# The last graph layer's adjacency product in whole fp32 instead of split fp32r

## The chip, the cores and the metric

The kernel runs on one core of a Trainium2 chip. The metric is the device time of one execution in microseconds. The core has TensorE (matrix products), VectorE (DVE), ScalarE (ACT), GpSimd (POOL), SyncE (SP, which here issues most transfers) and 16 DMA engines.

## What is computed

Four graph layers over 4096 nodes with 128 features each, and one dense 4096 x 4096 adjacency matrix `adj`. Each layer is a residual step on `h = relu(layernorm(x))`. The fourth, whose last part this case is about, is:

```
d = 1 / sqrt(sum(A, axis=-1))
z = leaky_relu(d[:, None] * (A @ (d[:, None] * x)) @ W1 + b1, 0.1)
S = exp(-sqrt(max(|z_i - z_j|^2, 0) + 1e-10) / 2), kept for the 4 nearest of each row, else 0
A2 = S + A
out = d2[:, None] * (A2 @ (d2[:, None] * x)) @ W2 + b2, with d2 = 1 / sqrt(sum(A2, axis=-1))
x = x + out
```

So each layer multiplies by `adj` once, and the fourth twice: once for `z`, and once more ("the last layer" below) for `out`, where four gathered neighbour rows are added to each row.

## The kernel before

**Visits.** The adjacency matrix is streamed from HBM in units of 512 KB: 256 rows of the contraction (two k-tiles of 128) by 512 output columns. TensorE's work on one unit is a *visit* (`Visit`, `visit(v)`). The ring in SBUF has `SLOTS` = 10 units; SP loads a unit as soon as TensorE has used the one ten visits before (`load_unit`, semaphore `used`). A block is 512 nodes (`NB` = 8 blocks), and a block of a layer takes `UNITS` = 16 visits, accumulated in one PSUM bank out of four.

**Split and whole.** A *whole* visit multiplies the ring's fp32 data by an fp32 operand (`G_first` or `G_last`) in one matmul per k-tile (line 429; the trace shows two records for one such matmul). A *split* visit has ScalarE round the unit to fp32r (`upper`, A_hi, tile staged in six buffers), VectorE subtract it from the data (`lower`, line 1066, A_lo, written over the ring's slot), and TensorE do three fp32r matmuls per k-tile (lines 424 to 426: hi x hi, hi x lo, lo x hi). The operand is split as well: `G_hi` by ScalarE and `G_lo` by VectorE.

**The search.** Between the product for `z` and the last layer, TensorE computes the 4096 distances of each of 32 row tiles (lines 599 to 603), ScalarE moves them out as `scores` (two halves of 2048, two buffers), and VectorE scans each tile twice (MAX8, line 1142, and FIND_INDEX8, line 1144). Once in four tiles VectorE also does `clamp`, `new_degrees`, `new_inverse` and `last_rest`, and ScalarE `similarity`, `new_roots` and `scale_last`. `scale_last` multiplies the rows `G_last` by the new inverse roots, which is the operand of the last layer; in the kernel before it also makes G_odd_hi, and `last_rest` (line 1169) makes G_odd_lo.

**The last layer.** Its 128 visits start when the last scores are out of PSUM. Block 0 is multiplied whole, since VectorE is still scanning; in blocks 1 to 7 the visits 7 and 15 are whole and the other 14 split, so 98 split visits and 30 whole. `G_last` is stored to HBM (`scaled_rows`), and when the eight stores have landed and the scans are done, GpSimd issues 128 indirect transfers (line 1246), four for each of 32 row tiles, into `landing`, which has slots for eight tiles. ScalarE scales the four rows (`scale_neighbours`, 16 instructions for a block's four tiles), VectorE adds them (`weigh`, lines 1177 and 1179), and this frees the slot. When a block's visits are done, ScalarE moves the bank out (`move_out`, at the fourth visit of the next block in its own order), TensorE transposes it (`natural`, line 462), and VectorE finishes the block's rows (`last_rows`, lines 1185 to 1193). SP stores them.

**Order.** Every engine works in the order in which its instructions are written. `near_due` says behind which visit a tile's `scale_neighbours` and `weigh` stand; it comes from three constants, of which `LAST_US` stands for a visit's time and `NEAR_US` for a tile's gathers. In the kernel before the tiles 27 to 31 fall due behind the last visit.

Of the kernel before, what the change touches and what calls it, by code (L numbers as in the profile page):

```python
# [58 lines left out]

WHOLE_BESIDE_SCANS = tuple(range(UNITS))  # L60
WHOLE_LAST = (7, 15)

LAST_US, NEAR_US, NEAR_FIRST = 1.5, 6.1, 9.0


class Plan:


    def __init__(self):
# [24 lines left out]
        for n in range(UNITS * NB):  # L96
            b, j = n // UNITS, n % UNITS
            u = j if b else (NB - 1 - j // HALVES) * HALVES + j % HALVES
            self.visits.append(Visit(len(self.visits), b, u, (4,), j not in (WHOLE_BESIDE_SCANS, WHOLE_LAST)[b > 0]))
            self.spans.setdefault((4, b, 4), [len(self.visits) - 1, 0])[1] = len(self.visits) - 1  # L100
# [4 lines left out]
        for t in range(NT):  # L105
            at = min(UNITS + int((NEAR_FIRST + NEAR_US * t) / LAST_US), UNITS * NB)
            self.near_due.setdefault(self.rows_end + at, []).append(t)
# [81 lines left out]
def gnn_stack(nc, x_in, at_in, pack_in, scaled_rows, out):  # L189
# [4 lines left out]
    with ctx:  # L194
# [11 lines left out]
        def take(name, kib):  # L206
# [97 lines left out]
            sem("clamp_ready"), sem("dist_ready"), sem("simil_ready"), sem("deg2_ready"), sem("root2_ready"))  # L304
        last_ready, lasthi_ready, lastlo_ready = sem("last_ready"), sem("lasthi_ready"), sem("lastlo_ready")
        zss_ready, negsq_ready = sem("zss_ready"), sem("negsq_ready")
# [65 lines left out]
        def _(pe):  # L372
# [17 lines left out]
            def operand_of(v, q, p):  # L390

                kb = v.u // HALVES
                if q == 0 and v.split:
                    pe.wait_ge(firstlo_ready, NB - 1)
                elif q == 0:
                    pe.wait_ge(first_ready, kb + 1)
                elif q < 4:
                    pe.wait_ge(g_ready, nth_h(q - 1, kb) - NB)
                elif v.b == 0:
                    pe.wait_ge(lastlo_ready if v.split else last_ready, NB - kb)  # L400
                else:
                    pe.wait_ge(lastlo_ready, NB)

            def visit(v):
# [11 lines left out]
                for q in v.feeds:  # L416
                    acc, odd = ps[:, PLAN.bank[q, v.b, p], :], 1 if q == 4 else q % 2
                    first, last = PLAN.spans[q, v.b, p]
# [218 lines left out]
        def _(act):  # L637
# [209 lines left out]
            def scale_last(m):  # L847
# [6 lines left out]
                last.then_inc(last_ready, 1)  # L854
                act.wait_ge(last_ready, m + 1)
                f(flat(G_hi[1], b), flat(G_last, b), ACT.Copy).then_inc(lasthi_ready, 1)

# [24 lines left out]
            for j, v in enumerate(PLAN.visits[PLAN.rows_end:]):  # L882
                if v.split:
                    upper(v)
                if v.b and j % UNITS == 3:
# [9 lines left out]
        def _(dve):  # L895
# [268 lines left out]

            def last_rest(m):

                b = seek_blocks[m]
                dve.wait_ge(lasthi_ready, m + 1)
                v_.tensor_tensor(flat(G_lo[1], b), flat(G_last, b), flat(G_hi[1], b).bitcast(fp32),
                                 ALU.subtract).then_inc(lastlo_ready, 1)  # L1170

            def weigh(t):
# [22 lines left out]
            for i in range(NT - 2):  # L1195
# [5 lines left out]
                elif i >= TPB and i % TPB == 1:  # L1201
                    new_inverse(i // TPB - 1)
                elif i >= TPB:
                    last_rest(i // TPB - 1)
            m = NB - 1
            scan(NT - 2)
            last_rest(m - 1)
            scan(NT - 1)
            clamp(m)
            new_degrees(m)  # L1210
            new_inverse(m)
            last_rest(m)
            for v in PLAN.visits[PLAN.rows_end:]:
                if v.split:
                    lower(v)
                for t in PLAN.near_due.get(v.n, ()):
# [68 lines left out]
```

## Time and profile before

| | us |
|---|---|
| median of 3 runs | 1427.42 (1427.2 to 1427.92) |
| profiled execution | 1424.98 |
| its span, first to last instruction | 1423.2 |
| TensorE busy | 1323.2 (93%) |
| VectorE busy | 1180.9 (83%) |
| ScalarE busy | 782.4 (55%) |
| GpSimd busy | 171.0 (12%) |
| mean granted clock of TensorE | 0.977 |
| search stage | 909 to 1187 |
| last layer's visits on TensorE | 1187.25 to 1396.74 |

Matmuls are pipelined, so a record of a matmul is longer than the spacing of two of them; the time of many is read from start to start. The shares of busy time are means over stages with different limits, so the stages have to be read one by one. An instruction's idle time before it, and who ended it, stand in brackets in a timeline.

### The profile page before, as it was taken

The page shows a single profiled execution, that of the slowest core. Times are in us where ns is not written, and L with a number is a line of the kernel's source. Part 1 is how long each engine was busy: PE and PEld are TensorE (multiplying, and loading weights), DVE is VectorE, ACT ScalarE, POOL GpSimd, SP SyncE. Part 2 cuts the span into 40 slices and gives each one's busy share as a digit, 9 for nine tenths or more (in the row PEclk, how much of TensorE's full clock was granted, in tenths as well). Part 3 has the DMA queues.
Part 4 walks back from the last instruction along what each step waited for, and adds up shares of the span by engine and source line. Part 5 has one row for each costly group of instructions (what it writes and reads, how often), then busy time and mean ns, then how long its engine had stood idle before and what let it go on. Part 6 is the DMA issues. An engine that isn't in the chain of part 4 may idle for free.

```text
span 1423.2 us, 15672 instructions
## 1 busy us (share of the span) xinstructions
PE 1323.2 (93%) x5508; PEld 951.0 (67%) x5508; DVE 1180.9 (83%) x1606; ACT 782.4 (55%) x1107; POOL 171.0 (12%) x144
## 2 busy tenths in 40 slices
PE   7999999999899999999999899899989999989992
PEld 4556677788678767777787777555555654667661
DVE  7987888898999878666558998599999998687883
ACT  2322232446666668665547686455555554676772
POOL 0000000000000000000000000000000000788885
PEclk9999999999999999999999999999999999999996
DMA  9787766558676776665557799100000004999991
GB/s 339 239 261 238 224 207 203 182 188 293 246 242 229 275 254 205 208 209 192 179 184 280 265 333 342 72 0 8 8 8 8 8 8 164 373 336 377 388 358 57
DMA packets 82862, 291.49 MB, mean 205 GB/s; under 512 B 10849, under 2 KB 10977, under 8 KB 82785
## 3 DMA queue, kind: packets, MB, share of 16 engines
q1 hardware_dynamic: 78048, 280.01, 56.6%
q0 software_dynamic: 4736, 10.49, 2.3%
q8 instruction: 44, 0.72, 0.2%
q14 instruction: 34, 0.27, 0.1%
HBM read 286.27 MB, written 4.19 MB: 204 GB/s over the span
## 4 chain that ended last, share of the span: by engine, by line
PE 51%; DVE 29%; POOL 9%; issue 5%; ACT 3%; DMA 2%; SPq 0%; POOLq 0%; ACTq 0%; DVEq 0%
PE ps L424 11%; PE ps L426 11%; PE ps L425 11%; POOL landing L1246 9%; DVE best_at L1144 9%; PE ps L429 9%; DVE rows_T L1142 9%; DVE A_lo L1066 6%; DMA landing<-scaled_rows,best_at 1%; PE ps L499 1%; PE ps L527 1%; PE ps L528 1%; PE ps L462 1%; PE ps L468 1%; DVE hn L916 1%
## 5 line engine op out<-in xcount | busy, mean ns | idle before, releaser
L1066 DVE TENSOR_TENSOR A_lo<-ring,A_hi 128x1024 fp32r<-128x1024 f32 x422 | 498.2, 1220 | 62.4 <-ACT A_hi L639 60.9
L639 ACT ACTIVATE A_hi<-ring 128x1024 fp32r<-128x1024 f32 x422 | 430.3, 1054 | 107.1 <-PE ps L426 96.6
L424 PE MATMUL ps<-A_hi,G_odd_hi 128*128 128x512 f32 x708 | 289.4, 409 | 15.6 <-DVE A_lo L1066 15.6
L426 PE MATMUL ps<-A_hi,G_odd_lo 128*128 128x512 f32 x708 | 278.5, 393 | 0.0
L425 PE MATMUL ps<-A_lo,G_odd_hi 128*128 128x512 f32 x708 | 278.3, 393 | 0.0
L1246 POOL DMA_INDIRECT landing<-scaled_rows,best_at x128 | 164.2, 1283 | 43.8 <-issue 37.5
L424 PEld LDWEIGHTS ps<-A_hi,G_odd_hi 128*128 128x128 f32 x708 | 134.3, 190 | 50.1 <-issue 14.5
L639 ACT ACTIVATE scores<-ps,neg_sq 128x2048 f32<-128x2048 f32 x64 | 124.4, 1964 | 62.9 <-PE ps L603 44.7
L425 PEld LDWEIGHTS ps<-A_lo,G_odd_hi 128*128 128x128 f32 x708 | 134.6, 190 | 29.8 <-issue 3.3
L426 PEld LDWEIGHTS ps<-A_hi,G_odd_lo 128*128 128x128 f32 x708 | 134.4, 190 | 29.2
L424 PE MATMUL ps<-A_hi,G_even_hi 128*128 128x512 f32 x368 | 153.5, 417 | 0.2 <-DVE A_lo L1066 0.2
L1238 POOL DMA_DIRECT2D scaled_rows<-G_last x8 | 6.2, 780 | 1199.2 <-ACT G_last L639 1199.2
L1142 DVE MAX8 rows_T<-scores 128x8 f32<-128x4096 f32 x32 | 141.3, 4415 | 9.5 <-ACT scores L639 9.5
L426 PE MATMUL ps<-A_hi,G_even_lo 128*128 128x512 f32 x368 | 143.6, 390 | 0.0
L425 PE MATMUL ps<-A_lo,G_even_hi 128*128 128x512 f32 x368 | 143.4, 390 | 0.0
L1144 DVE FIND_INDEX8 best_at<-rows_T,scores 128x8 uint32<-128x4096 f32 x32 | 141.4, 4419 | 0.0
L946 DVE TENSOR_TENSOR colsum<-colsum,ring 128x1024 f32<-128x1024 f32 x112 | 133.4, 1220 | 0.0
L429 PE MATMUL ps<-ring,G_first 128*128 128x512 f32 x288 | 128.8, 593 | 0.0
L601 PE MATMUL ps<-z_hi 128*128 128x512 f32 x256 | 111.5, 436 | 0.0
L602 PE MATMUL ps<-z_lo,z_hi 128*128 128x512 f32 x256 | 105.0, 410 | 0.0
L603 PE MATMUL ps<-z_hi,z_lo 128*128 128x512 f32 x256 | 104.7, 409 | 0.0
L429 PEld LDWEIGHTS ps<-ring,G_first 128*128 128x128 f32 x288 | 53.1, 191 | 58.5 <-issue 57.9
(136 smaller groups left out, 1367.1 us busy)
## 6 DMA issues: line engine op xcount, KB each, us to landing
ring<-adj_t SPq DMA_DIRECT2D x524, 512.0 KB, 4.8
X<-x_rows SPq DMA_DIRECT2D x8, 256.0 KB, 7.1
scaled_rows<-G_last POOLq DMA_DIRECT2D x8, 256.0 KB, 2.7
landing<-scaled_rows,best_at POOLq DMA_INDIRECT x128, 5.6
out_rows<-X SPq DMA_DIRECT2D x8, 256.0 KB, 5.2
pack<-packed SPq DMA_DIRECT2D x1, 836.0 KB, 14.5
pack<-packed SPq DMA_DIRECT2D x1, 192.0 KB, 4.1
```

The lines of the kernel that those rows point to most:

```text
L424: mm(acc, G_hi[odd][:, kb, t, :], hi, start=start, stop=False)
L425: mm(acc, G_hi[odd][:, kb, t, :], lo, start=False, stop=False)
L426: done = mm(acc, G_lo[odd][:, kb, t, :], hi, start=False, stop=stop)
L429: done = mm(acc, G[:, kb, t, :], ring[:, s, k, :], start=start, stop=stop)
L601: mm(ps[:, bank_of(c), :], hi, z_hi[:, c, :], start=False, stop=False)
L602: mm(ps[:, bank_of(c), :], hi, z_lo[:, c, :], start=False, stop=False)
L639: return nc.scalar.activation(out_ap, in_ap, func, **k)
L946: ins = v_.tensor_tensor(half, half, ring[:, s, :, :], ALU.add)
L1066: v_.tensor_tensor(A_lo[:, s, :, :], ring[:, s, :, :], A_hi[:, slot_of(v), :, :].bitcast(fp32), ALU.subtract).then_inc(lower_ready, 1)
L1142: own.add(v_.max(best[:, t, :], row))
L1144: v_.max_index(best_at[:, t, :], best[:, t, :], row).then_inc(scanned, 1)
L1246: pool.indirect_dma_start(out=landing[:, k, r, :], out_offset=None, in_=scaled_rows, in_offset=bass.IndirectOffsetOnAxis(ap=best_at[:, t, ...
```

## The change

All 128 visits of the last layer are whole. With that go the splitting of its operand (the ScalarE copy in `scale_last`, `last_rest` on VectorE and their two semaphores), the splitting of the units (`upper` and `lower` for these visits), and the selection of whole visits by two tuples. All visits now wait for `last_ready`. `LAST_US` and `NEAR_US` are other numbers, and a tile's due visit has a lower bound: six visits into the block behind its own, `UNITS * (t // TPB + 1) + 6`. Four tiles, 28 to 31, fall due behind the last visit. `operand_of` and `visit` are simplified to match.

```
-LAST_US, NEAR_US, NEAR_FIRST = 1.5, 6.1, 9.0
+LAST_US, NEAR_US, NEAR_FIRST = 1.75, 5.2, 9.0
...
-            self.visits.append(Visit(len(self.visits), b, u, (4,), j not in (WHOLE_BESIDE_SCANS, WHOLE_LAST)[b > 0]))
+            self.visits.append(Visit(len(self.visits), b, u, (4,), False))
...
-            at = min(UNITS + int((NEAR_FIRST + NEAR_US * t) / LAST_US), UNITS * NB)
+            at = max(UNITS + int((NEAR_FIRST + NEAR_US * t) / LAST_US), UNITS * (t // TPB + 1) + 6)
+            at = min(at, UNITS * NB)
...
-                elif v.b == 0:
-                    pe.wait_ge(lastlo_ready if v.split else last_ready, NB - kb)
-                else:
-                    pe.wait_ge(lastlo_ready, NB)
+                else:
+                    pe.wait_ge(last_ready, NB - kb if v.b == 0 else NB)
...
                 last.then_inc(last_ready, 1)
-                act.wait_ge(last_ready, m + 1)
-                f(flat(G_hi[1], b), flat(G_last, b), ACT.Copy).then_inc(lasthi_ready, 1)
...
             for j, v in enumerate(PLAN.visits[PLAN.rows_end:]):
-                if v.split:
-                    upper(v)
                 if v.b and j % UNITS == 3:
                     move_out(4, v.b - 1)
...
-            def last_rest(m):
-
-                b = seek_blocks[m]
-                dve.wait_ge(lasthi_ready, m + 1)
-                v_.tensor_tensor(flat(G_lo[1], b), flat(G_last, b), flat(G_hi[1], b).bitcast(fp32),
-                                 ALU.subtract).then_inc(lastlo_ready, 1)
...
-                elif i >= TPB:
-                    last_rest(i // TPB - 1)
...
             for v in PLAN.visits[PLAN.rows_end:]:
-                if v.split:
-                    lower(v)
                 for t in PLAN.near_due.get(v.n, ()):
```

VectorE in the search, round the third scan of a group of four, before. MAX and MAX_INDEX are one scan.

```order
L1163 RECIPROCAL d2inv<-root 128x4
L1142 MAX rows_T<-scores_54 128x8
L1144 MAX_INDEX best_at<-rows_T,scores_54 128x8
L1169 TENSOR_TENSOR G_odd_lo<-G_last,G_odd_hi 128x512
L1142 MAX rows_T<-scores_55 128x8
```

The same place now:

```order
L1154 RECIPROCAL d2inv<-root 128x4
L1133 MAX rows_T<-scores_54 128x8
L1135 MAX_INDEX best_at<-rows_T,scores_54 128x8
L1133 MAX rows_T<-scores_55 128x8
```

The 128x512 subtraction between two scans is gone; nothing else moves on this engine in the search.

ScalarE at the end of the last layer, before: A_hi is the rounding of a unit, rows_T the `move_out`, landing the scalings of gathered rows.

```order
L639 ACTIVATE A_hi<-ring 128x1024 x4
L639 ACTIVATE rows_T<-ps 128x512
L639 ACTIVATE landing<-landing,simil 128x128 x4
L639 ACTIVATE A_hi<-ring 128x1024 x3
L639 ACTIVATE landing<-landing,simil 128x128 x4
L639 ACTIVATE A_hi<-ring 128x1024 x4
L639 ACTIVATE landing<-landing,simil 128x128 x4
L639 ACTIVATE A_hi<-ring 128x1024 x3
L639 ACTIVATE landing<-landing,simil 128x128 x4
L639 ACTIVATE rows_T<-ps 128x512
L639 ACTIVATE landing<-landing,simil 128x128 x20
```

The same stretch now:

```order
L634 ACTIVATE rows_T<-ps 128x512
L634 ACTIVATE landing<-landing,simil 128x128 x16
L634 ACTIVATE rows_T<-ps 128x512
L634 ACTIVATE landing<-landing,simil 128x128 x16
L634 ACTIVATE rows_T<-ps 128x512
L634 ACTIVATE landing<-landing,simil 128x128 x16
```

The roundings are gone, and the 16 scalings of a block stand behind that block's `move_out` and before the next one. Behind the last `move_out` there are 16 scalings instead of 20.

TensorE in the last layer now, from its start (x40 is block 0 and four visits of block 1; the 128x128 rows are `natural`):

```order
L424 MATMUL ps<-ring,G_last 128x512 x40
L457 MATMUL ps<-pack,rows_T 128x128 x4
L424 MATMUL ps<-ring,G_last 128x512 x30
L457 MATMUL ps<-pack,rows_T 128x128 x4
L424 MATMUL ps<-ring,G_last 128x512 x32
```

Two matmuls a visit stand where six stood in the split visits; the transposes keep their place behind the third or fourth visit of the next block.

## Rows read from the trace of the kernel before

**Rows 1.** Stretches: length; busy PE, PEld, DVE, ACT, POOL (instructions); clock, DMA share, GB/s.
```profile
909.00:1187.00 278.00, 253.19 (x988) 159.78 (x986) 275.89 (x127) 154.00 (x128) 4.74 (x6) 0.96 0.02 6
...
1214.40:1397.00 182.60, 169.02 (x674) 126.75 (x672) 141.86 (x184) 127.80 (x210) 148.47 (x113) 0.97 0.95 350
1397.00:1423.20 26.20, 0.66 (x4) 0.42 (x4) 8.71 (x22) 6.64 (x21) 13.29 (x15) 0.58 0.19 58
...
1310.00:1350.00 40.00, 37.72 (x158) 28.57 (x157) 31.22 (x40) 27.72 (x47) 32.38 (x26) 1.00 1.02 391
```

**Rows 2.** Timeline of TensorE: last layer's first visits and last (start, us, instruction).
```profile
1187.25 27.73 PE L429 MATMUL ps<-ring,G_last 128*128 128x512 f32 x64 [2.06 <-ACT scores L639]
...
1215.05 0.39 PE L425 MATMUL ps<-A_lo,G_odd_hi 128*128 128x512 f32 x1
...
1394.86 1.88 PE L429 MATMUL ps<-ring,G_last 128*128 128x512 f32 x4
```

**Rows 3.** Timeline of GpSimd: the first gather, one near the end, the last.
```profile
1211.61 1.80 POOL L1246 DMA_INDIRECT landing<-scaled_rows,best_at  x1 [5.13 <-DMA scaled_rows<-G_last]
...
1406.13 0.94 POOL L1246 DMA_INDIRECT landing<-scaled_rows,best_at  x1 [0.30 <-issue]
...
1413.61 0.95 POOL L1246 DMA_INDIRECT landing<-scaled_rows,best_at  x1 [0.30 <-issue]
```

**Rows 4.** Timeline of ScalarE and VectorE at the end of the span.
```profile
1396.78 0.60 ACT L639 ACTIVATE rows_T<-ps 128x512 f32<-128x512 f32 x1 [4.90 <-PE ps L429]
1397.27 1.26 ACT L639 ACTIVATE landing<-landing,simil 128x128 f32<-128x128 f32 x4
...
1416.07 1.28 ACT L639 ACTIVATE landing<-landing,simil 128x128 f32<-128x128 f32 x4 [3.59 <-DMA landing<-scaled_rows,best_at]
...
1420.06 0.69 DVE L1193 TENSOR_TENSOR X<-X,nat 128x512 f32<-128x512 f32 x1
```

**Rows 5.** VectorE in the search: a group (count, busy, idle before), then its timeline.
```profile
L1142 DVE MAX8 rows_T<-scores 128x8 f32<-128x4096 f32 x32 | 141.3, 4415 | 9.5 <-ACT scores L639 9.5
...
972.24 0.67 DVE L1169 TENSOR_TENSOR G_odd_lo<-G_last,G_odd_hi 128x512 fp32r<-128x512 f32 x1
972.83 4.42 DVE L1142 MAX8 rows_T<-scores 128x8 f32<-128x4096 f32 x1
```

**Rows 6.** Timeline of ScalarE at the end of the search.
```profile
1182.12 1.98 ACT L639 ACTIVATE scores<-ps,neg_sq 128x2048 f32<-128x2048 f32 x1 [2.73 <-DVE best_at L1144]
1185.23 1.97 ACT L639 ACTIVATE scores<-ps,neg_sq 128x2048 f32<-128x2048 f32 x1 [1.14 <-PE ps L603]
...
1204.16 1.28 ACT L639 ACTIVATE G_last<-G_last,d2inv 128x128 f32<-128x128 f32 x4 [0.24 <-DVE d2inv L1163]
```

**Rows 7.** Timeline of TensorE in the first layer: transposes and whole visits.
```profile
62.38 0.60 PE L468 MATMUL ps<-pack,hn 128*128 128x128 f32 x4
62.82 1.88 PE L429 MATMUL ps<-ring,G_first 128*128 128x512 f32 x4
...
65.43 13.90 PE L429 MATMUL ps<-ring,G_first 128*128 128x512 f32 x32
...
79.39 0.40 PE L425 MATMUL ps<-A_lo,G_even_hi 128*128 128x512 f32 x1
```

**Rows 8.** Timeline of TensorE in the last layer: split visits, six records apart.
```profile
1313.15 0.39 PE L426 MATMUL ps<-A_hi,G_odd_lo 128*128 128x512 f32 x1
...
1314.51 0.39 PE L426 MATMUL ps<-A_hi,G_odd_lo 128*128 128x512 f32 x1
```

**Rows 9.** Waits from 1214.4 to 1397 us: in total, times, longest.
```profile
ACT landing L639 <- DMA landing<-scaled_rows,best_at: 46.3, 25, 4.7
...
PE ps L424 <- DVE A_lo L1066: 13.3, 8, 2.5
```

**Rows 10.** Timeline of VectorE and GpSimd over the same stretch.
```profile
1299.29 4.62 DVE L1066 TENSOR_TENSOR A_lo<-ring,A_hi 128x1024 fp32r<-128x1024 f32 x4
...
1300.49 1.97 POOL L1246 DMA_INDIRECT landing<-scaled_rows,best_at  x1 [0.30 <-issue]
```

More of the change, by code:

```diff
@@ L57 @@
 FILL = 6
-WHOLE_BESIDE_SCANS = tuple(range(UNITS))
-WHOLE_LAST = (7, 15)
-LAST_US, NEAR_US, NEAR_FIRST = 1.5, 6.1, 9.0
+LAST_US, NEAR_US, NEAR_FIRST = 1.75, 5.2, 9.0
 class Plan:
@@ L304, in gnn_stack @@
             sem("clamp_ready"), sem("dist_ready"), sem("simil_ready"), sem("deg2_ready"), sem("root2_ready"))
-        last_ready, lasthi_ready, lastlo_ready = sem("last_ready"), sem("lasthi_ready"), sem("lastlo_ready")
+        last_ready = sem("last_ready")
         zss_ready, negsq_ready = sem("zss_ready"), sem("negsq_ready")
@@ L416, in visit @@
                 for q in v.feeds:
-                    acc, odd = ps[:, PLAN.bank[q, v.b, p], :], 1 if q == 4 else q % 2
+                    acc, odd = ps[:, PLAN.bank[q, v.b, p], :], q % 2
                     first, last = PLAN.spans[q, v.b, p]
@@ L1202, in _ @@
                     new_inverse(i // TPB - 1)
-                elif i >= TPB:
-                    last_rest(i // TPB - 1)
             m = NB - 1
             scan(NT - 2)
-            last_rest(m - 1)
             scan(NT - 1)
@@ L1211, in _ @@
             new_inverse(m)
-            last_rest(m)
             for v in PLAN.visits[PLAN.rows_end:]:
-                if v.split:
-                    lower(v)
                 for t in PLAN.near_due.get(v.n, ()):
```

## The prediction

> **What bounds the kernel now.** I read the busy times by stage first, then the chain that ended last, then the timelines round its joints, and the waits last. The change lives in the last two stages. In the similarity search (909 to 1187 us) the reader is to see VectorE at 275.89 of 278 us and TensorE's granted clock at 0.96 [rows 1]: VectorE paces it. From 1187.25 us the last layer's 128 visits run on TensorE until 1396.74, and then nothing matters on TensorE for 26.5 us more: the last stretch has 0.66 us of matmuls [rows 1, 2]. What is late there is GpSimd: its 128 gathers start at 1211.61 and the last one at 1413.61, one every (1413.61 - 1211.61) / 127 = 1.59 us, and the end is that gather's landing, four scalings, 3.4 us of VectorE and the last store [rows 3, 4]. So two strands run side by side, TensorE up to 1396.7 and GpSimd up to 1413.6, and GpSimd decides. The change moves both, so each must be laid out in absolute time.
>
> **Part 1: the splitting of the operand goes (search stage).** `last_rest` leaves VectorE's queue. It stands alone between two scans: 0.67 us long, but from its start to that of the next MAX8 it is 0.59 us (972.24 to 972.83) [rows 5]. Six of the eight (blocks ranked 0 to 5) lie before the scan whose end lets ScalarE move out the last row's scores from 1182.12 on [rows 6]; TensorE's first visit waits for ScalarE there [rows 2]. VectorE waits for scores only once, 9.5 us at the start of the stage [rows 5], so the six are on the path: 6 x 0.59 = 3.5 us. TensorE's visits then begin at 1187.25 - 3.5 = 1183.7. The seventh lies before the last scan, so the last `scale_last` and the start of the gathers come 7 x 0.59 = 4.1 us earlier: 1211.61 - 4.1 = 1207.5. The eighth, and the eight ScalarE copies of 0.63 us (ScalarE is busy 154 of 278 us there [rows 1]) cost nothing now and give nothing; each stands behind the scaling of G_last for which GpSimd waits. Block 0's visits need the last operand rows at visit 14, 1183.7 + 14 x 1.72 = 1207.7, and these are ready at 1205.44 - 4.1 = 1201.3; covered by 6 us.
>
> **Part 2: TensorE's visits.** A whole visit is two fp32 matmuls, four records. In the first layer 32 such records run from 65.43 until 79.39 less one split record (0.23), so 13.73 / 32 = 0.429 us each at granted clock 1.00, 1.716 us a visit [rows 2, 7]. Block 0 of the last layer shows the same: 64 records between 1187.25 and 1215.05 - 0.23, 0.431 each [rows 2]. A split visit at full clock is six records in 1.36 us (1313.15 to 1314.51) [rows 8]. So each of the 98 visits that change costs TensorE 0.36 us more, 35 us in all. But it did not run at that pace: of the 181.8 us from 1214.8 to 1396.6, split work is 98 x 1.36 = 133.3, whole work 14 x 1.716 = 24.0 and seven groups of transposes 7 x 0.44 = 3.1 (62.38 to 62.82 [rows 7]), 160.4 together; 21.4 us are stall and half clock. The waits name it: TensorE waits 13.3 us for A_lo, and ScalarE, which must make A_hi first and works in its own order, 46.3 us for landed gathers [rows 9]. The new visits wait for the ring's transfer and no engine. So the new stretch is 128 x 1.716 + 3.1 = 222.8 us and TensorE ends at 1183.7 + 222.8 + 0.2 (the last record outlasts the spacing) = 1406.7, 10 us later than now.
>
> A rule of the skill speaks against the change here. The Trainium skill ("FP8 and Floating Point Precision", TensorE Precision Notes) says that true fp32 takes four passes through the array, and the split form has three. The rows agree, 1.716 / 1.36 being 1.26. By the rule alone the change would be about 31 us slower, by the rows 5 us faster; what the kernel would need for the former is the fourth rival below.
>
> **Part 3: the gathers.** A gather takes 0.94 us plus 0.30 to the next while VectorE is mostly idle (1406.13), and 1.97 when it lies under a run of the subtractions (1299.29, four in 4.62 us) [rows 3, 10]. With the 98 subtractions gone only the sums and row updates remain on VectorE, 3.4 us at a block's end [rows 4]. I take 1.25; the bounds are 1.24 and today's 1.59. The Trainium skill ("SBUF — State Buffer", Who interferes with whom) says that a VectorE instruction with two SBUF inputs contends with GpSimd's reads; by that the gathers would keep the short price except under `weigh`, and the 1.97 beside the subtractions agrees. With 1.25 the last gather would issue at 1207.5 + 127 x 1.25 = 1366. The new due times make ScalarE scale a block's tiles only behind its `move_out`, and a landing slot is free eight tiles later: tile 28 waits for tile 20, so for block 5, which ends at 1183.7 + 6 x 27.9 = 1351. Its last gathers then run from about 1353 to 1373 and land by 1379 (5.6 us). That is 28 us of cover before TensorE ends.
>
> **Part 4: the new tail.** The last block's four tiles are due only after the last `move_out`, so the 16 scalings stand behind it though their data landed long before. Today the last `move_out` starts 0.04 us behind TensorE and the first scaling 0.49 us behind that; four scalings take 1.28, their starts 0.30 apart [rows 4], so sixteen take 15 x 0.30 + 0.39 = 4.9. From the end of the last scaling (1417.35) to the end of the span is 5.85 us: the last tile's two sums, `last_rows` and the store [rows 4]. The new tail is 0.04 + 0.49 + 4.9 + 5.85 = 11.3 us, where today it is 26.5. The span ends at 1406.7 + 11.3 = 1418.0.
>
> **Part 5: edits with one answer.** The store of a block is due 12 visits behind its tiles; SP waits for it with up to ten visits loaded ahead, and by the times above a block's rows are final 5 to 6 us before SP asks. ScalarE's natural order (16 scalings, `move_out`) holds TensorE's transposes, three visits (5 us) behind the block's end, by nothing: the scalings of the block before were done 15 us or more earlier, except block 0's, by 5.
>
> **The sum.** Start -3.5, visits +13.5 (TensorE's end moves from 1396.7 to 1406.7), tail 11.3 - 26.5 = -15.2: -5.2 us. The profiled span is 1423.2 us, its execution 1424.98, 2.4 below the median of 1427.42; I take the difference to the median: 1422.2 us.
>
> **The rivals.**
> - *The transfers set the pace (slower).* New demand: 0.524 MB a visit / 1.716 = 306 GB/s, gathers 65.5 KB / 1.25 us = 52, stores 9: 367 GB/s for some 165 us. For: the share is 0.95 over the stretch and 1.02 in its fastest part. Against: 391 GB/s were carried for 40 us on end, gathers among them [rows 1]. The ring's ten slots are full at the start (5.2 MB), which covers 32 GB/s of shortfall, so it decides from a sustained 335 downwards; at 320 it costs (47 x 165 us - 5.2 MB) / 320 = 8 us: 1430, and with it TensorE's stalls and half clock (0.97 granted today) could come back.
> - *The search gives nothing back (same).* If TensorE at half clock (1.2 GHz, some of the time at 0.96 granted [rows 1]) becomes what VectorE waits for, the 3.5 us go: 1425.7. Against it stands that VectorE never waits after its first scan.
> - *The gathers still end last (faster).* At 1.59 each they issue until 1207.5 + 127 x 1.59 = 1409.4, and the end shifts by the 4.1 us alone: 1423.3. Against: the 0.94 us rows.
> - *TensorE was the bound (slower).* Then the tail stays and the end is 1406.7 + 26.5 = 1433.2 in span, 10 us slower (1437); if the stalls stayed too, the whole 98 x 0.36 - 3.5 = 32 us (1459). Against: 21.4 us of stall and a tail whose chain is GpSimd. The case needs the last gathers to issue after 1395, 20 us later than they can.
>
> **How the numbers follow.** Forecast 0.64; search gives nothing 0.12; gathers 0.06; transfers 0.07; TensorE or the tail 0.03; and 0.08 for a start up to 2 us earlier still (the last scores wait 1.14 us for TensorE today [rows 6]), 1420. About 0.2% (2.9 us) is what can be told from no change. Faster than 1424.6 are the forecast nearly whole, the gathers and the early start: 0.77. Same: the search case and a little of the forecast, 0.14. Slower 0.09. The range reaches from 1419.8 (early start) to 1426.8 (search gives nothing, and a microsecond of the transfers).
>
> **What would show it.** Right: TensorE's first last-layer matmul near 1183.7; its records 0.43 apart without a gap, clock 1.00 until 1406.7; gathers mostly 0.94 to 1.0 us and all landed by 1385; the chain ending in TensorE's visits, then sixteen scalings in 4.9 us; a tail of 11.3 us. Wrong: matmuls of the last layer that wait for the ring or start at half clock (transfers); waits of the MAX8 on scores (search); a chain through the gathers (gathers).

## The result, and the profile after

| | before | after |
|---|---|---|
| median of 4 executions each, us | 1427.31 (1424.08 to 1427.92) | 1454.91 (1451.96 to 1458.19) |
| ratio, 95% interval | | 1.0199 (1.0178 to 1.022) |
| profiled execution, span | 1424.98, 1423.2 | 1458.19, 1456.4 |

The change was measured 27.6 us slower where 5.2 us faster was forecast. Experiments further down show that this holds for some chips and not for others: on another chip the same kernel took 1423.02 us against 1426.78. Both results have to be explained, and the slow one comes first.

One stretch of the kernel before, and then the stretches of the changed kernel in this first result, with the columns of [rows 1]:

```profile
1227.00:1275.00 48.00, 42.06 (x168) 31.60 (x167) 37.85 (x52) 33.62 (x55) 39.02 (x30) 0.96 0.97 363
```

```profile
1187.00:1212.00 25.00, 25.00 (x59) 11.13 (x60) 13.14 (x8) 5.63 (x13) 1.94 (x3) 1.00 0.79 279
1212.00:1227.00 15.00, 15.00 (x40) 6.82 (x39) 0.77 (x2) 2.99 (x9) 11.34 (x13) 1.00 0.97 334
1227.00:1275.00 48.00, 27.04 (x48) 9.78 (x46) 4.69 (x12) 2.72 (x9) 33.75 (x36) 0.69 0.37 112
1240.00:1270.00 30.00, 12.02 (x16) 3.61 (x15) 0.00 (x0) 0.00 (x0) 22.69 (x25) 0.58 0.35 106
```

The loss sits in one place. From 1227 to 1275 us the DMA engines are busy to 0.37 and move 112 GB/s, where the kernel before had 0.97 and 363. From 1240 to 1270 TensorE runs 16 matmul records in 30 us instead of some 70 (30 / 0.43), and its granted clock falls to 0.58 behind the gaps. VectorE and ScalarE do nothing at all. Only GpSimd keeps its pace, 25 gathers in 30 us.

TensorE's timeline over its onset and end (start, us, instruction, idle before and releaser), to set beside [rows 2]:

```profile
1186.95 34.60 PE L424 MATMUL ps<-ring,G_last 128*128 128x512 f32 x80 [2.06 <-ACT scores L634]
1221.82 20.54 PE L424 MATMUL ps<-ring,G_last 128*128 128x512 f32 x47
1243.88 0.59 PE L424 MATMUL ps<-ring,G_last 128*128 128x512 f32 x1 [1.51 <-issue]
1246.68 1.01 PE L424 MATMUL ps<-ring,G_last 128*128 128x512 f32 x1 [2.21 <-issue]
...
1257.18 1.01 PE L424 MATMUL ps<-ring,G_last 128*128 128x512 f32 x1 [1.79 <-issue]
1259.98 1.01 PE L424 MATMUL ps<-ring,G_last 128*128 128x512 f32 x1 [1.79 <-issue]
```

A gap that ends in "issue" is one in which the engine waited for nothing that the profile shows. Most records come 2.80 us apart here, a few 2.10, also within one visit, where the program has no wait. And the data were in the ring: by the transfers' own packets the unit of the visit that starts at 1257.18 was complete by 1246. So no data held a matmul back, and the engine still had none to run. SyncE is late as well, and earlier. Its waits from 1212 to 1412 us (total, times, longest), and its timeline:

```profile
SPq L341 <- PE ps L424: 59.6, 37, 4.7
SPq L341 <- remote: 44.9, 5, 10.9
```

```profile
1223.73 58.13 SPq L341 DMA_DIRECT2D ring<-adj_t  x13
1281.91 0.44 SPq L345 DMA_DIRECT2D out_rows<-X  x1
```

"Remote" on one core means that no releaser was found. These five loads start 7.0 to 11.2 us apart from 1225.66 on (1232.68, 1242.49, 1252.98, 1264.18, 1275.38), although TensorE had used their slots 6 to 42 us before; from 1278.90 on six follow within 2.6 us. SyncE's lateness alone would have cost most of the loss: the load of 1275.38 is for the 37th visit, which at 0.43 us a record would have started near 1249.6, by my estimate, some 26 us before that. GpSimd's timeline has the event that ends it:

```profile
1211.56 1.02 POOL L1224 DMA_INDIRECT landing<-scaled_rows,best_at  x1 [5.95 <-DMA scaled_rows<-G_last]
...
1270.47 0.94 POOL L1224 DMA_INDIRECT landing<-scaled_rows,best_at  x1 [0.30 <-issue]
1281.95 0.94 POOL L1224 DMA_INDIRECT landing<-scaled_rows,best_at  x1 [10.53 <-DVE near L1163]
```

The first 48 gathers follow each other 1.25 us apart without a pause. At 1271.4 the slots are full and GpSimd stops; SyncE's loads follow each other again from 1278.90 and TensorE's matmuls from 1280.70, 7.5 and 9.3 us later. In [rows 3, 10] the subtractions stretched the gathers to 1.59 us in the mean, and until the visits ended at most five in a row kept 1.25.

The visits therefore end at 1445.24 (the last 52 records start at 1422.76 and take 22.48), 258.3 us after their start instead of the 223.0 forecast. The tail has its forecast shape, where [rows 4] had 20 us of gathers and four scalings in front:

```profile
1445.28 0.60 ACT L634 ACTIVATE rows_T<-ps 128x512 f32<-128x512 f32 x1 [22.65 <-PE ps L424]
1445.77 4.77 ACT L634 ACTIVATE landing<-landing,simil 128x128 f32<-128x128 f32 x16
```

### The profile page after: what moved, and what is told of

The parts are those of the page before. It is cut to its first block, busy times and chain, and to the rows that moved or that the text cites. A ratio compares the mean times of both kernels' runs of the same rounds, so it can differ in the third digit from the quotient of the medians.

```text
span 1456.4 us, 14970 instructions
## 1 busy us (share of the span) xinstructions
PE 1367.5 (94%) x5312; PEld 917.9 (63%) x5312; DVE 1064.1 (73%) x1500; ACT 682.1 (47%) x1001; POOL 128.2 (9%) x144
## 4 chain that ended last, share of the span: by engine, by line
PE 61%; DVE 28%; another core or an unknown queue 3%; issue 3%; ACT 3%; DMA 2%; POOL 1%; SPq 0%; ACTq 0%; DVEq 0%; POOLq 0%
PE ps L424 20%; PE ps L419 10%; PE ps L421 10%; PE ps L420 10%; DVE best_at L1135 9%; DVE rows_T L1133 8%; DVE A_lo L1057 6%; PE ps L494 1%; PE ps L522 1%; PE ps L523 1%; PE ps L457 1%; POOL landing L1224 1%; PE ps L463 1%; ACT A_hi L634 1%
## 5 line engine op out<-in xcount | busy, mean ns | idle before, releaser
L1057 DVE TENSOR_TENSOR A_lo<-ring,A_hi 128x1024 fp32r<-128x1024 f32 x324 | 383.8, 1218 | 57.4 <-ACT A_hi L634 56.0
L634 ACT ACTIVATE A_hi<-ring 128x1024 fp32r<-128x1024 f32 x324 | 333.7, 1056 | 104.1 <-PE ps L421 93.4
L424 PE MATMUL ps<-ring,G_last 128*128 128x512 f32 x512 | 231.0, 608 | 24.1 <-issue 22.0
L419 PE MATMUL ps<-A_hi,G_odd_hi 128*128 128x512 f32 x512 | 204.7, 400 | 2.1 <-DVE A_lo L1057 2.1
L421 PE MATMUL ps<-A_hi,G_odd_lo 128*128 128x512 f32 x512 | 200.2, 391 | 0.0
L420 PE MATMUL ps<-A_lo,G_odd_hi 128*128 128x512 f32 x512 | 199.8, 390 | 0.0
L424 PEld LDWEIGHTS ps<-ring,G_last 128*128 128x128 f32 x512 | 98.8, 194 | 150.3 <-issue 147.9
L1224 POOL DMA_INDIRECT landing<-scaled_rows,best_at x128 | 121.4, 949 | 85.6 <-DVE near L1163 42.5
L421 PEld LDWEIGHTS ps<-A_hi,G_odd_lo 128*128 128x128 f32 x512 | 96.4, 188 | 20.7
L420 PEld LDWEIGHTS ps<-A_lo,G_odd_hi 128*128 128x128 f32 x512 | 96.6, 189 | 19.3 <-issue 0.5
```

The source lines that it names most:

```text
L419: mm(acc, G_hi[odd][:, kb, t, :], hi, start=start, stop=False)
L420: mm(acc, G_hi[odd][:, kb, t, :], lo, start=False, stop=False)
L421: done = mm(acc, G_lo[odd][:, kb, t, :], hi, start=False, stop=stop)
L424: done = mm(acc, G[:, kb, t, :], ring[:, s, k, :], start=start, stop=stop)
L634: return nc.scalar.activation(out_ap, in_ap, func, **k)
L1057: v_.tensor_tensor(A_lo[:, s, :, :], ring[:, s, :, :], A_hi[:, slot_of(v), :, :].bitcast(fp32), ALU.subtract).then_inc(lower_ready, 1)
```

## The experiments

Times are of one execution where nothing else is said. The kernels of one session ran on one chip beside the kernel before; the chips carry numbers here. Two more variants, one with a quarter of the gathers and one without the lower bound on the due times (one run of nearly 128 gathers), have no time, so what they were to show isn't measured. The theory at the start: unbroken gathers at 1.25 us hold up SyncE and TensorE. Its rivals: too much demand on the transfers, and an idle engine or its clock as the cause.

### Pauses between the gathers (chip 2)

```
+                if t >= TPB and t % TPB == 0:
+                    pool.wait_ge(used, PLAN.rows_end + UNITS + 14 * (t // TPB))
```

> The changed kernel with all gathers, but GpSimd starts each block's 16 gathers only behind visit 16 + 14 m, so no run is longer than 16 gathers (20 us) and 4 us lie between two. Theory A (a long unbroken run): TensorE keeps 0.43 us a record throughout, at most SyncE is late by some us at the end of each run, which the ring's ten slots hide; span 1418 to 1421. Theory B: the stall of 35 us at 1242 to 1277 stays, span about 1455. Theory C (too much transfer work in total): the same bytes, so the stall stays or is spread, span 1440 or more.

Measured: 1423.0 us, beside 1429.14 for the kernel before; no gap between TensorE's visits above 0.8 us. The demand on the transfers is the same, so it isn't the cause. SyncE is still late at the end of some groups of 16 (20 us long); the last figure is its longest wait, and on the chips without the slow stretch no such wait is above 1.8:

```profile
SPq L341 <- PE ps L424: 80.8, 43, 8.4
```

The ring's ten units (17 us of visits) cover it.

### The gathers later (chip 2)

```
+            pool.wait_ge(used, PLAN.rows_end + 2 * UNITS)
```

> The changed kernel with the first gather held back until 32 visits of the last layer are done (about 1242 us instead of 1211). Theory A: the slow stretch moves with the gathers; it begins some 16 us behind the first gather, near 1258 for SyncE and 1272 for TensorE, and ends behind the first long run; since more tiles are free of their slots late, the run may be longer or shorter, the span 1430 to 1460. Theory B (something at a fixed place of the program, such as a refill of instructions): it begins at 1227 to 1242 as now.

Measured: 1483.13 us. The slow stretch moved with the gathers. They start at 1243.99 now, and the stretches (columns of [rows 1]) show full pace before them and the crawl behind:

```profile
1227.00:1243.00 16.00, 16.00 (x39) 7.09 (x38) 0.00 (x0) 0.00 (x0) 0.00 (x0) 1.00 0.88 297
1243.00:1288.00 45.00, 26.10 (x60) 11.74 (x59) 8.63 (x23) 10.70 (x33) 33.42 (x35) 0.77 0.43 140
1288.00:1330.00 42.00, 15.60 (x17) 4.21 (x15) 2.20 (x6) 0.00 (x0) 27.46 (x29) 0.54 0.32 97
```

18.9 us of the middle one are another matter: TensorE waits for `rows_T`, which ScalarE moves out behind scalings whose gathers come late. SyncE stands still too, from 1245 to 1270, for the store of those rows. So the onset was not 16 us behind the first gather, as expected: SyncE is first late from about 1273 (the load of 1275.86 by 2.8 us, the next by 12.4) and TensorE from 1288.56, 29 and 45 us behind the first gather, with some 20 us in between in which neither had anything to do.

### A slower pace (chip 14)

```
+                    g.memset(filler[:, :], 0.0).then_inc(filled, 1)
+                    pool.wait_ge(filled, TOPK * t + r + 1)
```

(behind each gather; `filler` is 128x128)

> The changed kernel with a small GpSimd memset behind every gather, which adds some 0.3 to 0.5 us to the spacing of two gathers (1.25 us now, 1.59 on average in the kernel before) while the run of gathers stays as unbroken as it was. Theory A1, the rate of the gathers does it: with 1.6 us or more between them SyncE and TensorE are not slowed at all; the gathers end last, near 1211 + 127 x 1.6 = 1414 us or later, and the span is 1425 to 1450 us with no matmul 2.8 us behind another. Theory A2, the length of the run without a pause does it, whatever the rate: the slow stretch lasts until the slots run out, 48 gathers x 1.6 = 77 us instead of 60, and the span is 1465 us or more.

Measured: 1420.39 us beside 1429.57, span 1418.5, the forecast's 1418.0. GpSimd's timeline, and the stretch that was slow:

```profile
1229.18 0.95 POOL L1225 DMA_INDIRECT landing<-scaled_rows,best_at  x1 [0.27 <-issue]
1230.13 0.22 POOL L1229 MEMSET filler<- 128x128 f32 x1
1230.62 0.95 POOL L1225 DMA_INDIRECT landing<-scaled_rows,best_at  x1 [0.27 <-issue]
```

```profile
1227.00:1275.00 48.00, 48.00 (x120) 21.61 (x119) 10.80 (x28) 11.30 (x34) 38.69 (x67) 1.00 0.99 359
```

At 1.44 us from gather to gather all 128 run on for 186 us, no two of them more than 2.1 us apart, and nobody is late.

### More landing slots (chip 14)

```
-GSLOTS = 8
+GSLOTS = 16
```

> The changed kernel with 16 landing slots instead of 8, so GpSimd is held up later: the first run is 96 gathers or so (until about 1331 us) instead of 48 (until 1271). Theory A: the slow stretch is as much longer as the run, TensorE at 2.8 us a record from 1242 to about 1334, span 1490 to 1515 us. Theory B (a fixed stall of 35 us that is not tied to the run's length): span 1450 to 1460. Theory D (GpSimd being held up is what costs): more slots mean fewer hold-ups, span near 1420.

Measured: 1498.63 us. The first unbroken run lasts until 1308.3, and so does the slow stretch: SyncE's loads come 10 to 11 us apart until 1315.

```profile
1243.00:1288.00 45.00, 16.17 (x16) 4.88 (x17) 0.00 (x0) 0.00 (x0) 34.03 (x37) 0.50 0.33 99
```

A buffer that lets GpSimd run further ahead makes it worse: 69 us above the kernel before on this chip, where the changed kernel with 8 slots was 27 to 28 above it on two others. In the changed kernel the full slots are what ends the harm.

### Plain transfers in place of gathers (chip 14)

```
-                    pool.indirect_dma_start(...)
+                    pool.dma_start(landing[:, k, r, :], scaled_rows[P * t:P * (t + 1), :]).then_inc(gathered[k], 16)
```

(the rows come in order, so this kernel doesn't add the nearest ones)

> The changed kernel with the 128 gathers replaced by 128 plain transfers from GpSimd's queue of the same size (128 rows of 512 bytes each, rows in order, so the rows that are added are not the nearest ones). It tells whether the indirect addressing or any run of transfers issued by GpSimd slows SyncE and TensorE. Theory A3, the work of making descriptors in software: plain transfers of 128 rows each need the same number of them and slow the two in the same way, from some 16 us into the run or earlier; span 1440 us or more. Theory A4, only the indirect ones (reading indices, addresses in software): no slow stretch, TensorE's visits in 223 us, span 1416 to 1421.

Measured: 1419.98 us, no slow stretch. The transfers go out 0.53 us apart, so 48 of them take only 25 us, and then 10 to 20 us pass before each burst of 16. The runs are too short to tell much.

### Pauses, and an earlier last block (chip 14, then chip 5)

```
-            at = min(at, UNITS * NB)
+            at = min(at, UNITS * NB - 7)
...
+                if t >= 4 and t % 4 == 0:
+                    pool.wait_ge(used, PLAN.rows_end + 16 + 13 * (t // 4))
```

(and the last store stays behind all loads)

> A version meant to be faster than both: the changed kernel with each block's 16 gathers started 13 visits behind the last block's (22.3 us for a run of 20 us, first at visit 16), and with the last block's 16 scalings and sums due seven visits before the end instead of behind it (the last two stores stay behind all loads). Theory A: no stall of TensorE, its visits take 223 to 225 us from about 1184 to 1408, and the tail is 4.8 us shorter than the 11.1 of the paced run: 6.3 us. Span 1414 to 1417 us, some 10 us below the kernel before on the same chip. If pauses of 2.3 us are too short for SyncE to catch up, TensorE starves of data in places and the span is above 1420.

Measured: 1416.17 us beside 1429.57. The same kernel again, four times, on chip 5:

> The paced kernel again (groups of 16 gathers start behind visit 16 + 13 per group, last block's tiles due seven visits before the end), now timed in rounds. Theory: 1416, ratio 0.991 to 0.993, and every round within a microsecond or two of it, since each run of 16 gathers delays SyncE by less than the ring's ten units cover. Rival (pacing only makes the slow stretch less likely): single rounds 20 us and more above the fastest.

Measured: 1415.57 us (1414.63 to 1416.9, 4 executions) beside 1427.49, ratio 0.9918 (0.9896 to 0.9939). The four executions bear the theory out, but SyncE's waits (same view as above, first chip 14, then chip 5) brought the first sign against it:

```profile
SPq L341 <- PE ps L424: 98.3, 49, 11.3
```

```profile
SPq L341 <- PE ps L424: 135.1, 99, 1.8
```

One and the same kernel has waits up to 11.3 us on one chip and none above 1.8 on the other. I took notice of that only after the next two groups.

### What stands between two gathers (chip 5)

The 1.44 us pace with the earlier last block; the clearing of one column (`g.memset(filler[:, n:n + 1], 0.0)`, no wait) behind each gather; and a clearing of 128x512 with a wait behind every fourth.

> The changed kernel with three edits: behind each gather GpSimd clears 128x128 and waits for that (1.44 us from gather to gather instead of 1.25, no other pause), the last block's tiles fall due seven visits before the last visit instead of behind it, and the last store stands behind all loads. Theory (the harm comes from gathers issued without a break of their own, and nothing else of the change costs time): no slow stretch of TensorE; the earlier due time takes the sixteen scalings (4.8 us) out of the tail, 11.1 to about 6.5; 1420.4 - 4.6 = 1416, ratio to the kernel before 0.991. Rival (the length of the unbroken run counts, and the one profile without a slow stretch was luck): in some rounds 1450 and more, a median near 1440.

> The changed kernel, with a clearing of one column (128x1, in its own column of a buffer) behind each gather and no wait for it. It puts another instruction of GpSimd between two gathers but adds only a little time, by my estimate 0.1 us, so that they follow each other at 1.3 to 1.35 us. Theory R (the rate decides: above some rate the gathers' work queues up and SyncE and TensorE are held): the slow stretch is still there, shorter or milder, 1440 to 1458. Theory B (what decides is that GpSimd does something else, or waits, between two gathers): no slow stretch, 1419 to 1421.

> The changed kernel, with one clearing of 128x512 and a wait for it behind every fourth gather: three gathers of four follow at 1.25 us, and then comes a break of, by my estimate from the 128x128 one (0.22 us), 0.6 to 0.9 us. The mean spacing is about that of the kernel with a clearing behind each gather (1.44). Theory R (the mean rate decides): no slow stretch, 1419 to 1421. Theory B (each single break must be there): gathers in threes may do harm, but a run of four is far shorter than the 16 us after which SyncE first fell behind, so 1419 to 1421 as well unless what the gathers leave behind adds up over the breaks: then 1440 to 1458.

Measured: 1415.32 us over four executions (1414.82 to 1417.72, ratio 0.992, 0.9898 to 0.9942), 1424.01 and 1422.13. None has a slow stretch. The second keeps the gathers at 1.25 us, 112 of them in a row, so I dropped the pace as the cause and took the instruction between them. That was a wrong turn, since nothing on this chip had shown the harm without it.

### Fewer and fewer edits (chip 3)

A column cleared behind every 32nd gather; `filler` only allocated and cleared once at the program's start; a wait for a long-reached semaphore ahead of each gather; and the column behind each gather, with the earlier last block.

> The changed kernel, with a clearing of one column (128x1) behind every 32nd gather only. Theory B (gathers with nothing else of GpSimd between them bring SyncE and TensorE to a crawl after some 16 us, and another instruction of GpSimd ends that): the gathers' first run is 48 long, so the crawl starts near 1227 as in the changed kernel and ends with the clearing near 1250 instead of 1276: some 23 us of it instead of 49, 1458 - 16 to 22 = 1436 to 1442. Rival C (the clearings matter for something else, the first runs' luck or where the buffer lies): either no crawl at all (1420 to 1424) or the whole of it (1452 to 1458).

> The changed kernel with the buffer that the clearings write to, cleared once at the program's start, and no clearing between gathers. Theory B: the slow stretch is there in full, 1452 to 1458, TensorE at 2.8 us a record from about 1242 to 1276. Rival C (it is the buffer's 512 bytes per partition, which shift what lies behind them in SBUF): 1419 to 1424.

> The changed kernel with a wait ahead of each gather, for a semaphore that has long had its value. It tells whether GpSimd has to do work between two gathers or only to handle a semaphore. Theory B in its narrow form (a working instruction is needed): 1452 to 1458 with the slow stretch. In its wide form (anything that stands between two gathers will do): 1419 to 1424.

> The changed kernel with the clearing of one column behind each gather, and the last block's tiles due seven visits before the end. Theory B: no slow stretch in any round, and as fast as the kernel with clearings of 128x128 and a wait, 1415.3: 1414 to 1417, ratio 0.991 to 0.993. Rival (the single run at 1424.0 without a slow stretch was luck): a median above 1430 or rounds of 1450.

Measured: 1423.48, 1422.51 and 1423.39 us, and over four executions 1416.49 (1415.83 to 1417.85, ratio 0.992, 0.9901 to 0.9939). None has a slow stretch. One clearing 1200 us before the gathers cannot do what 128 between them do. The placement in SBUF that the buffer shifts isn't it either, since the kernel with the waits leaves it as it was. What remains is that the kernel didn't decide it at all.

### The changed kernel itself again (chip 13)

> The changed kernel itself, unchanged, beside the kernel before on whatever chip this is. Theory K (what stands in GpSimd's stream or in SBUF decides whether SyncE and TensorE are held up): 1452 to 1458 in every round, as in its first four executions, with the slow stretch from 1227 to 1276. Theory D (the kernel has nothing that decides it; the chip or how the program was placed on it does, since the clearing once at the start and the waits made as much difference as a clearing behind every gather, and all seven kernels of the last two jobs, on two other chips, ran without a slow stretch): 1419 to 1424 here, ratio 0.995 to 0.998, or, on a chip of the first kind, 1452 to 1458 for it and for the next kernel too.

> The kernel with the buffer and one clearing at the program's start again, on the same chip as the changed kernel itself. Theory K: 1419 to 1424, while the changed kernel is at 1452 to 1458. Theory D: both alike, both at 1419 to 1424 or both at 1452 and more.

Measured: the unchanged kernel 1423.02 us (1420.81 to 1426.11, 10 executions) beside 1426.78 (1423.77 to 1431.93, 13), ratio 0.9968 (0.9953 to 0.9984); the kernel with the buffer 1420.66. Theory D, that nothing in the kernel decides it, holds. TensorE's timeline and the stretch of its profiled execution (1421.48 us, span 1419.7):

```profile
1185.48 34.60 PE L424 MATMUL ps<-ring,G_last 128*128 128x512 f32 x80 [2.06 <-ACT scores L634]
...
1246.54 27.63 PE L424 MATMUL ps<-ring,G_last 128*128 128x512 f32 x64
...
1386.07 22.48 PE L424 MATMUL ps<-ring,G_last 128*128 128x512 f32 x52
```

```profile
1227.00:1275.00 48.00, 48.00 (x119) 21.61 (x118) 11.52 (x30) 12.35 (x39) 36.72 (x38) 1.00 1.00 364
```

It is the program of the first result, with 38 gathers in the same 48 us (36 there), and nobody is held up.

### Both on one more chip (chip 6)

> The changed kernel itself once more, on whatever chip this is. Theory D (the chip or the session decides whether the slow stretch comes): either 1420 to 1426 without it, as on the last chip, or 1452 to 1458 with it. It tells how to read the next kernel.

> The kernel with a clearing of one column behind each gather, at an unchanged 1.25 us from gather to gather, on the same chip as the changed kernel itself. If that one shows the slow stretch here: 1419 to 1424 for this one if a clearing between two gathers is what kept the 1.44 us kernel free of it, 1440 to 1458 if the slower pace did. If that one is free of it here: 1420 to 1425, and the question stays open.

Measured: 1455.96 and 1455.11 us beside 1429.37. The slow stretch is back, and the cleared column does next to nothing against it (the stretch of that kernel):

```profile
1227.00:1275.00 48.00, 30.46 (x50) 10.44 (x48) 3.95 (x10) 2.55 (x8) 35.93 (x69) 0.75 0.40 118
```

GpSimd's timeline of this kernel adds something: with two instructions per gather GpSimd is itself late for a while.

```profile
1246.91 0.11 POOL L1230 MEMSET filler<- 128x1 f32 x1
1247.21 0.94 POOL L1225 DMA_INDIRECT landing<-scaled_rows,best_at  x1 [0.19 <-issue]
1248.16 0.11 POOL L1230 MEMSET filler<- 128x1 f32 x1
1249.03 0.94 POOL L1225 DMA_INDIRECT landing<-scaled_rows,best_at  x1 [0.76 <-issue]
1250.91 0.10 POOL L1230 MEMSET filler<- 128x1 f32 x1 [0.94 <-issue]
```

So three engines are late in the slow stretch with nothing that they wait for. That speaks for something that brings them their instructions, and against the matmul array, the ring or a DMA engine's time. It isn't shown: the transfers that refill instructions are as many in the trace of the first result as in that of chip 13 (86 packets), and around the stretch none took longer than 1.4 us in either.

### What the chips say together

| chip | kernels | slow stretch | landing records of the gathers, of 2048 |
|---|---|---|---|
| of the first result | kernel before; changed kernel (4 executions) | none; in all four, by their times | 2048; 301 |
| 2 | pauses; gathers later | SyncE waits up to 8.4 us; full | 410; 343 |
| 14 | 1.44 us pace; 16 slots; plain transfers; pauses | none; full; none; SyncE waits up to 11.3 us | 1312; 321; 2048; 301 |
| 6 | changed kernel; cleared column | full; full | 328; 269 |
| 5, 3, 13 | ten kernels, the changed one (10 executions) among them | none | 2048 in all ten |

The table is one of chips, but it may as well be one of sessions on them: each numbered chip was used in one session, and the first result's carries no number. Shown is that the same program has the slow stretch on one and not on another, and that its executions in one session agree. The kernel before is no guide to the kind of chip: 1427.3, 1429.1, 1429.6 and 1429.4 us on the first kind, 1427.5, 1427.4 and 1426.8 on the second, where single executions spread from 1421 to 1432.

The last column parts the two kinds as well. A transfer that lands leaves 16 records in the trace, so 128 gathers leave 2048. On chips 5, 3 and 13 every trace has all of them. On the others most are missing wherever gathers follow at 1.25 us, over a third where they follow at 1.44, and none in the kernel before (1.59 in the mean) or with plain transfers. The same holds for the ring's loads, so that the view of the transfers (issues, KB, median us to landing) has no median in the first result and has one on chip 13:

```profile
ring<-adj_t SPq DMA_DIRECT2D x118, 512.0 KB
landing<-scaled_rows,best_at POOLq DMA_INDIRECT x128
```

```profile
ring<-adj_t SPq DMA_DIRECT2D x118, 512.0 KB, 5.6
landing<-scaled_rows,best_at POOLq DMA_INDIRECT x128, 5.4
```

In the first result 19 records of gathers are left from 5 to 10 us behind the first gather, where chip 13 has 66, and SyncE isn't late before 15 us. So the loss of records is no consequence of the late loads. It comes first, it grows with the pace, and the kernel with 1.44 us shows it without any harm. What writes the records may be what holds the engines up, or both may suffer from a third thing; the runs don't part these. (A releaser whose record is missing can't be named either, which may be all that "remote" says above.)

On chips of the first kind, what the kernel does still counts. The slow stretch comes with indirect gathers at 1.25 us, SyncE falls behind some 13 to 16 us into an unbroken run (29 us in the kernel with later gathers, where it had stood still for 25), and the stretch moves with the run, lasts as long and ends behind it. At 1.44 us it did not come, and a cleared column at 1.25 us did not keep it away. That the pace is what counts rests on two different chips of the first kind (14 and 6; 14 had the slow stretch with 16 slots) and on one execution each, and the 1.44 us kernel also waits for its clearing each time; it is likely, not shown.

Why the engines are late is open. No view shows what they wait for, nor why only some chips have it. The missing records make the recording itself a suspect; but every execution of this case was recorded by the profiler, so no run tells whether the slow stretch is there without it.

## Why the prediction was wrong, point by point

**Part 1 (3.5 us from the search) was right.** MAX8 of the first scan to MAX8 of the last but one takes 272.28 us in the trace of before and 268.65 in both traces of the changed kernel: 3.63 less.

**Part 2 (a visit in 1.716 us, nobody in the way) failed on chips of the first kind, and was right on the other one that ran this kernel.** On chip 13 the visits take from 1185.48 to 1386.07 + 22.48 = 1408.55, 223.07 us where 222.8 + 0.2 was forecast, at clock 1.00. In the first result they take 258.3. The step that failed is the sentence that the new visits wait for the ring's transfer and no engine, with the overlap behind it: that gathers at 1.25 us run beside SyncE and TensorE without touching either. TensorE's records came 2.80 us apart with nothing to wait for, and SyncE's loads up to 43 us behind the use of their slots, 35.3 us in all. What made them late stays open.

**Part 3 (gathers at 1.25 us) was right as a price and wrong as a gift.** The price is 0.94 + 0.30 in both traces. On chip 13 they run as laid out: they stop for slots where expected, at tile 28, after 112 in a row without harm, start again at 1356.16 (forecast: 1353) and end at 1375.05 (forecast: 1373).

```profile
1349.64 0.94 POOL L1224 DMA_INDIRECT landing<-scaled_rows,best_at  x1 [0.30 <-issue]
1356.16 0.94 POOL L1224 DMA_INDIRECT landing<-scaled_rows,best_at  x1 [5.58 <-DVE near L1163]
```

The prediction read the subtractions only as something that slowed the gathers [rows 10], and their going as pure cover. That they also kept GpSimd from issuing 48 gathers at a stretch, and that this may have protected SyncE and TensorE, was not asked, and the trace of before has no row that shows it: it holds no unbroken run of more than five beside the visits.

**Part 4 (the tail) was right.** 1456.4 - 1445.28 = 11.1 us in the first result, and 11.1 on chip 13, for 11.3.

**Part 5 was right where the visits were.** On chip 13 SyncE never waits more than 1.8 us behind a visit, and TensorE's transposes stand in their places without a gap.

**The rivals.** The first had the right sign and even its marks, matmuls that start at half clock and a ring that isn't filled, but not its mechanism: the DMA engines were two thirds idle. On chip 13 they carry 364 GB/s for the 48 us shown at share 1.00, and no transfer holds a matmul up. The rule of four passes with its 31 us slower, and the fourth rival's 1459, come near the measured 1454.9 by coincidence: outside the slow stretch a visit costs its 1.716 us in both traces, the tail shrank to 11.1 us, and on chip 13 the same kernel is faster.

**The sum.** On chip 13 the medians differ by 3.8 us (1426.78 - 1423.02) for the forecast's 5.2, and the absolute 1423.02 lies 0.8 from the forecast's 1422.2; the interval of the ratio, 2.3 to 6.7 us, holds it. In the profiled executions the change is 1423.2 - 1419.7 = 3.5. The missing 1.7 are a first scan that starts at 911.7 instead of 909.8, in a part of the kernel that the change doesn't touch, less 0.2 in the tail; so the terms came out, and how near the medians came is in part luck, since single executions of one kernel here lie up to 9 us apart. Against the first result the whole error is one term of 35 us that the sum did not have: 258.3 - 223.0 in the visits, with 3.4 us of the same untouched part (first MAX8 at 913.16) on top of it.

## What to carry to other kernels

When a change takes work off an engine that slowed another, ask what the freed engine does at full speed and to whom. Here indirect gathers of GpSimd, back to back at 1.25 us, came with a loss of 35 us on some chips. Spread over the visits that they serve they cost nothing on either kind, and with a last block that falls due before the end that kernel takes 0.991 (1416.17 / 1429.57) and 0.992 of the time before. A buffer that lets an engine run further ahead is no gain if nobody needs the data yet. Ask also whether the trace is whole: records that are missing in one of two traces mark a difference before any time does. And a result that differs between two kernels on two chips isn't a difference of the kernels until both have run on one: four experiments here were spent on edits that did nothing.

## What the runs showed of the hardware

- A TensorE that waits for "issue" between matmuls, with its data in place, and a SyncE whose loads come 7 to 11 us apart with no releaser, mark one event. In it most matmul records come 2.80 us apart and the granted clock falls to 0.50 to 0.58 (0.50 with 16 slots, 0.54 with later gathers, 0.58 in the first result).
- SyncE falls behind first, near 1227 us, and TensorE some 15 us later, after 37 more records at full pace; the delay is about 15 us in all five traces with the full stretch, also where both had stood still before it. The Trainium skill ("TensorE: Matmul & The Clock Gate", the table at its head) gives TensorE a queue of 64 instructions. A record here goes with a weight load, so 64 instructions are 32 records, by my estimate 14 us of work at 0.43 us each; the delay of the trace is about that, and both engines may have been cut off at the same time. The runs don't show the queue itself.
- GpSimd's gathers keep their 1.25 us throughout the slow stretch as long as nothing else stands in GpSimd's stream.
- The same program, the changed kernel, has none of it in ten executions on one chip and all of it in five elsewhere.
- Where the event can come, landing records of transfers go missing from the first 5 to 10 us of the gathers on: 301 of 2048 are left in the first result, 1312 at a pace of 1.44 us, all on chips 5, 3 and 13.
